# Cross-attention and FFN on one core: the last pair shuffled like the others, and half-height queries and projections

## What is computed

```
kv_rope = kv_c * cos[None] + _rotate_half(kv_c) * sin[None]
q_hk = (hidden_q @ Wq.T).reshape(b, s, H, K)
q_big = jnp.einsum('bshk,hkq->bshq', q_hk, w_kc_q)
q_r = jnp.einsum('bshq,hqr->bhsr', q_big, W_qr)
k_r = jnp.einsum('bld,hdr->bhlr', kv_rope, W_kr)
scores = jnp.einsum('bhsr,bhlr->bhsl', q_r, k_r)
attn = jax.nn.softmax(scores, axis=-1)
ctx_c = jnp.einsum('bhsl,bld->bhsd', attn, kv_rope)
ctx_lat = jnp.einsum('bhsd,hkd->bshk', ctx_c, w_kc_kv)
out = ctx_lat.reshape(b, s, H * K) @ Wo.T
```

## Time and profile before

| | |
|---|---|
| median of 3 runs | 136.69 us (136.23 to 137.05) |
| the profiled execution | 136.4 us, its span 134.6 us |
| PE busy | 127.3 us (95%) |
| DVE busy | 105.7 us (79%) |
| ACT busy | 75.5 us (56%) |
| POOL busy | 85.5 us (64%) |
| the chain that ended last | PE 75%, DVE 9%, ACT 8%, DMA 4% |

### The profile page before, as it was taken

The page is one execution under the profiler, slowest core; times in us unless marked ns, Lnnn a source line. Parts: engine busy times, 40 slices in busy tenths (PEclk is TensorE's granted clock), DMA queues, the critical chain, the costliest instruction groups (busy, mean ns, idle before and its releaser), DMA issues.

```text
span 134.6 us, 2532 instructions
## 1 busy us (share of the span) xinstructions
PE 127.3 (95%) x910; PEld 90.5 (67%) x910; DVE 105.7 (79%) x159; ACT 75.5 (56%) x192; POOL 85.5 (64%) x126
## 2 busy tenths in 40 slices
PE   6989799999889999999999999999999999999992
PEld 6767589467657767666576676666675686766770
DVE  0387844999999684996999699699969799997092
ACT  4242643769459382937638475983976673544110
POOL 6507957969989939296957959677585643004240
PEclk9999999999999999999999999999999999999999
DMA  3899987999999799899989999999889980000004
GB/s 81 232 336 216 154 135 256 231 125 211 233 252 249 150 217 211 207 297 276 245 234 305 261 249 282 239 262 309 227 234 178 267 221 23 5 0 0 0 0 156
DMA packets 29132, 26.13 MB, mean 194 GB/s; under 512 B 17056, under 2 KB 20768, under 8 KB 29120
## 3 DMA queue, kind: packets, MB, share of 16 engines
q1 hardware_dynamic: 26992, 22.84, 69.3%
q0 software_dynamic: 1456, 2.77, 9.0%
q10 hardware_dynamic: 672, 0.36, 0.9%
HBM read 10.50 MB, written 0.52 MB: 82 GB/s over the span
## 4 chain that ended last, share of the span: by engine, by line
PE 75%; DVE 9%; ACT 8%; DMA 4%; SPq 1%; issue 1%; ACTq 0%; DVEq 0%
PE score L968 18%; PE ctxb L984 16%; PE ctxb L939 8%; PE proj L994 8%; ACT probs L451 6%; DVE neg_max L650 4%; PE score L1128 4%; DMA ctx_rows<-in_ctx_dram 4%; PE foldb L904 3%; PE foldb L919 3%; DVE turned L666 2%; PE score L1153 1%; PE score L1106 1%; PE foldb L1128 1%; PE ctxb L950 1%; DVE bulk L615 1%
## 5 line engine op out<-in xcount | busy, mean ns | idle before, releaser
L451 ACT ACTIVATE probs<-score,neg_max 128x512 f32<-128x512 f32 x64 | 43.2, 686 | 28.8 <-DVE neg_max L650 28.8
L389 POOL TENSOR_SCALAR probs<-probs,row_inv 128x512 f32<-128x512 f32 x64 | 43.9, 735 | 23.8 <-DVE row_inv L656 23.8
L650 DVE TENSOR_REDUCE neg_max<-score 128x2 f32<-128x1024 f32 x32 | 37.6, 1216 | 10.9 <-PE score L968 10.9
L968 PE MATMUL score<-k_t,q_t 64*128 64x256 f32 x256 | 32.7, 391 | 1.5 <-ACT probs L451 1.4
L666 DVE STREAM_TRANSPOSE turned<-probs 128x1024 f32<-128x1024 f32 x28 | 33.0, 1216 | 0.0
L968 PEld LDWEIGHTS score<-k_t,q_t 64*128 64x128 f32 x256 | 23.2, 186 | 8.9 <-ACT probs L451 3.7
L381 POOL DMA_DIRECT2D wo<-in_L_xattn_Wo_dram x32 | 28.0, 1019 | 0.0
L984 PE MATMUL ctxb<-spread,kv 128*64 128x256 f32 x192 | 22.0, 382 | 0.0
L984 PEld LDWEIGHTS ctxb<-spread,kv 128*64 128x64 f32 x192 | 13.3, 137 | 8.0 <-issue 2.0
L939 PE MATMUL ctxb<-hq_t,m 128*128 128x512 f32 x28 | 13.7, 611 | 0.0
L451 ACT ACTIVATION_READ_ACCUMULATOR probs<-score,neg_max 128x1 f32 x64 | 13.0, 203 | 0.0
(11 more groups left out here) (144 smaller groups left out, 149.3 us busy)
## 6 DMA issues: line engine op xcount, KB each, us to landing
spread<-turned SPq DMA_DIRECT2D x56, 256.0 KB, 5.5
wo<-in_L_xattn_Wo_dram POOLq DMA_DIRECT2D x32, 64.0 KB, 5.0
wq<-in_L_xattn_Wq_dram SPq DMA_DIRECT2D x1, 1280.0 KB, 13.7
bulk<-in_L_ffn_pweight_dram SPq DMA_DIRECT2D x2, 512.0 KB, 6.2
bulk<-in_L_ffn_nweight_dram SPq DMA_DIRECT2D x2, 512.0 KB, 7.2
bulk<-in_L_xattn_w_kc_q_dram SPq DMA_DIRECT2D x4, 192.0 KB, 8.7
wq<-in_L_xattn_Wq_dram SPq DMA_DIRECT2D x1, 512.0 KB, 7.4
wkv<-in_L_xattn_w_kc_kv_dram SPq DMA_DIRECT2D x1, 512.0 KB, 5.9
```

The costliest lines, as they stand in the source:

```text
L389: pool.tensor_scalar(p, p, row_inv[:, j:j + 1], 1.0, ALU.mult, ALU.mult).then_inc(norm_made, 1)
L451: act.activation(probs[:, j, :], score[u % 2][:, h, :], ACT.Exp, bias=neg_max[:, j:j + 1], accum_out=row_sum[:, j:j + 1]).then_inc(exp_mad ...
L650: dve.tensor_reduce(neg_max[:, j:j + 2], score[u % 2][:], axis=AX, op=ALU.max, negate=True)\
L968: product = pe.matmul(score[u % 2][:, h, half * S:half * S + S], q_t[rows, i % 2, b, tt * P:tt * P + P], k_t[rows, b, half * S:half * S + ...
```

## The change

1. `key_ident`, a permuted copy of the identity, is made once on POOL. The key transposes read it in place of a permuting access pattern on `ident`.
2. For pairs 3 to 6 `queries_and_projections(i)` replaces `queries(i + 1)` and `projections(i - 3)`. Each product is split into an upper and a lower half of 64 rows, like the scores. Two halves of different batches run as a couple into different banks: query batch 0 into ctx_bank, batch 1 into fold_bank. The second couple-set adds the other halves, after a wait on PE's own semaphores. ACT takes a query with two copies (`take_split_queries`).
3. The last pair is turned by DVE and shuffled by SP like all others; kv_turned, its four transfers, the PE transposes and their copies go.
4. The FFN's scales, bias and difference move from DVE to POOL, between the normalises of pairs 5 and 6. The weighted sum stays on DVE, split in `first_bits` and `last_bits`, for output half 0 in pair 6 and before pair 7, for half 1 at the end. `weight_tanh` of half 0 comes after pair 4 in place of pair 5. The loads of Wo come a pair earlier from pair 4 on.
5. PE's order after pair 7 is new.

The core of the diff:

```diff
-            for i in range(LASTP):
+            for i in range(NP):
                 for half in range(2):
                     spread_probs(i, half)
...
+            pool.wait_ge(ident_made, 1)
+            pool.tensor_copy(key_ident[:].rearrange("p (k c) -> p k c", k=G),
+                             ident[:].rearrange("p (c k) -> p k c", k=G)).then_inc(key_ident_made, 1)
...
+            def ffn_difference(ot):
+                pool.wait_ge(tanh_made, 2 * ot + 2)
+                pool.tensor_tensor(pw[:, ot, :], pw[:, ot, :], nw[:, ot, :], ALU.subtract).then_inc(difference_made, 1)
+
             for i in range(NP):
                 for half in range(2):
                     normalise(2 * i + half)
                     for j in range(K // BK):
                         if i == 0:
                             load_wo(half, j)
-                        elif i < LASTP and j // 2 == half:
-                            load_wo(i + 1, j)
+                        elif i < SECOND and j // 2 == half:
+                            load_wo(i + 1 if i < 3 else i + 2, j)
+                            if i == 2:
+                                load_wo(4, j)
+                    if i == 5 and half == 0:
+                        weight_scales()
+                    elif i == 5:
+                        ffn_difference(0)
+                    elif i == SECOND and half == 0:
+                        bias_values()
+                    elif i == SECOND:
+                        ffn_difference(1)
...
-                if i in (5, 6):
-                    act.wait_ge(ld_ffn[i - 5], 32)
-                    weight_tanh(2 * (i - 5))
-                    weight_tanh(2 * (i - 5) + 1)
+                if i in (4, 6):
+                    act.wait_ge(ld_ffn[(i - 4) // 2], 32)
+                    weight_tanh(i - 4)
+                    weight_tanh(i - 3)
...
+            def first_bits(ot):
+
+                dve.wait_ge(difference_made, ot + 1)
+                dve.wait_ge(scales_made, 1)
                 w_bits = pw[:, ot, :].rearrange("o (i n) -> o i n", n=NB)
                 link(dve.tensor_scalar(w_ffn[:, ot, :], w_bits[:, :, 0], bits[:, 3, 0:1], None, ALU.mult))
...
+                link(dve.scalar_tensor_tensor(w_ffn[:, ot, :], w_bits[:, :, 1], bits[:, 3, 1:2],
+                                              w_ffn[:, ot, :], ALU.mult, ALU.add))
...
             for i in range(1, LASTP):
                 u, v = SLOTS * i, 2 * i
+                if i == SECOND:
+                    first_bits(0)
                 maxima(u)
...
             u, v = SLOTS * LASTP, 2 * LASTP
+            last_bits(0)
             maxima(u)
...
             early_residual(T - 1)
+            first_bits(1)
+            last_bits(1)
...
+            def queries_and_projections(i):
+
+                p, old = i + 1, i - 3
+                upper, lower = slice(0, 64), slice(64, P)
+                query_bank = [ctx_bank[:, 0:S], fold_bank[:, 0:S]]
...
+                pe.wait_ge(long_taken, contexts_count(i - 1))
+                pe.wait_ge(fold_taken, values_count(i - 1))
+                for t in range(DT):
+                    query_part(upper, t, 0, t == 0)
+                    last = query_part(lower, t, 1, t == 0)
+                last.then_inc(query_half, 1)
+                for tt in range(TT):
+                    projection_part(upper, 0, tt, old == 0)
+                    last = projection_part(lower, 1, tt, old == 0)
+                last.then_inc(projection_half, 1)
+                pe.wait_ge(query_half, old + 1)
+                for t in range(DT):
+                    query_part(upper, t, 1, False)
+                    last = query_part(lower, t, 0, False)
+                last.then_inc(long_made, 1)
+                pe.wait_ge(projection_half, old + 1)
...
+                for tt in range(TT):
+                    projection_part(upper, 1, tt, False)
+                    last = projection_part(lower, 0, tt, False)
+                last.then_inc(projected_count, 1)
...
             values_side(LASTP)
-            late_contexts(SECOND, 0)
...
+            projections(LASTP - 2)
+            late_contexts(SECOND, 0)
+            late_contexts(SECOND, 1)
+            late_project(SECOND, 0)
+            late_project(SECOND, 1)
+            late_contexts(LASTP, 0)
             pe.wait_ge(ffn_w_made, DT)
+            pe.wait_ge(long_taken, contexts_count(LASTP))
...
+            late_project(LASTP, 0)
+            late_contexts(LASTP, 1)
             transpose_hidden(0)
             transpose_hidden(1)
-            late_contexts(LASTP, 1)
             ffn(0)
-            late_project_tile(1, 0)
-            late_project_tile(1, 1)
+            late_project(LASTP, 1)
             ffn(1)
```

More of the change, by code:

```diff
@@ L580, in _ @@
                .then_inc(ffn_w_taken, 1)
-            take_hidden(0)
-            take_hidden(1)
             take_late_contexts(LASTP, 1, 4)
-            take_hidden(2)
-            take_hidden(3)
+            for t in range(T):
+                take_hidden(t)
         @block.vector
@@ L656, in inverses, with turn_two @@
                 dve.reciprocal(row_inv[:, j:j + 4], row_sum[:, j:j + 4]).then_inc(inv_made, 1)
+            def turn_two(v, n):
+                i, half, j = v // 2, v % 2, 4 * (v % 2) + 2 * n
+                if i >= 2 and n == 0:
+                    dve.wait_ge(probs_spread[i % 2][half], landed(i - 2))
+                dve.wait_ge(norm_made, 4 * v + 2 * n + 2)
+                dve.transpose(turned[i % 2][:, :, j:j + 2, :, :].rearrange("p k j l r -> p (j l) k r"),
+                              probs[:, j:j + 2, :].rearrange("p j n -> p (j n)")).then_inc(probs_turned, 1)
@@ L696, in ffn_weights, with last_bits @@
+            def last_bits(ot):
+                w_bits = pw[:, ot, :].rearrange("o (i n) -> o i n", n=NB)
+                for n in range(2, NB):
+                    link(dve.scalar_tensor_tensor(w_ffn[:, ot, :], w_bits[:, :, n], bits[:, 3, n:n + 1],
+                                                  w_ffn[:, ot, :], ALU.mult, ALU.add))
                 link(dve.bn_stats(w_stats[:, ot, :], w_ffn[:, ot, :]))
@@ L1011, in projections, with half_height, query_part, projection_part @@
                 last.then_inc(projected_count, 1)
+            def half_height(bank, stationary, moving, start, stop):
+                return pe.matmul(bank, stationary, moving, start=start, stop=stop, skip_group_check=True)
+            def queries_and_projections(i):
+                p, old = i + 1, i - 3
+                upper, lower = slice(0, 64), slice(64, P)
+                query_bank = [ctx_bank[:, 0:S], fold_bank[:, 0:S]]
+                def query_part(rows, t, b, start):
+                    return half_height(query_bank[b], m[rows, p, t, :], hq_t[rows, t, b, :], start, t == DT - 1 and not start)
+                def projection_part(rows, b, tt, start):
+                    return half_height(out_bank[b][:, tt * D:tt * D + D], ctx_t[rows, (TT * b + tt) * P:(TT * b + tt) * P + P],
+                                       n_all[rows, old, :], start and tt == 0, False)
+                pe.wait_ge(long_taken, contexts_count(i - 1))
[9 more added lines that the diff above has]
+                pe.wait_ge(query_half, old + 1)
+                for t in range(DT):
+                    query_part(upper, t, 1, False)
[6 more added lines that the diff above has]
+                last.then_inc(projected_count, 1)
             turn_keys(0)
@@ L1077, in _ @@
                 scores(i, 1)
-                queries(i + 1)
-                projections(i - 3)
+                queries_and_projections(i)
                 scores(i, 2)
```

170 lines of the change are left out of this document (51 added, 119 removed).

## The result

| | before | after |
|---|---|---|
| median of 4 runs | 136.53 us (136.23 to 137.05) | 142.12 us (141.31 to 142.78) |
| the profiled execution | 136.4 us, span 134.6 us | 142.0 us, span 140.2 us |

The ratio is 1.041, with a 95% interval of 1.038 to 1.044. The direction was forecast, but 142.12 us lies above the range of 137.0 to 141.8, and 2.6 us above the 139.5 named. In some executions of a kernel the clock is lower and the time over 1.5% longer; the medians and ratios of the experiments leave these out.

A forecast was written before the change was run, and what follows sets the result against it. PE bounds pairs 3 to 6, with little DVE slack; then DVE, ACT and PE, finally nearly all PE. Terms +6.0 - 3.6 + 0 + 0.4 = +2.8 on 136.4 gave 139.2, as a median 139.5 us; range 137.0 to 141.8.

The forecast's parts named there:

- Part 4: Pair 6: first_bits(0) on DVE waits for POOL's FFN difference, PE stands 5.2 us, and maxima(28) come 6.0 us later.
- the clock: PE work after its stand in pair 6: the clock falls to the 1.2 GHz level, costing +0.4 us.
- Part 1: Key transposes with key_ident, before the first scores: 0.87 us less PE work, bounds 0 and 0.9.
- Part 2: Half-height products in pairs 3 to 6: no change of tiling around the block, saving 0.40 us for each pair.
- Part 3: weight_tanh moved from pair 5 to pair 4 on ACT: pair 5's block waits for n_all, 0.3 us lost.
- Part 5: The end, contexts(5) to late_contexts(7, 1): 15.8 us on PE instead of 19.4, so -3.6 us.
- I take it as hidden by PE: The last pair's shuffle, landing at 124.7 to 126.9, lies under PE's work to 126.0, with up to 0.9 us to pay.
- the late bound: Last pair's shuffle: the longest time from last turn to landing, put at 8.4 us, landing at 126.9.
- The tail: Behind the start of late_contexts(7, 1): added and removed PE work cancel, change 0, 10.9 us to the end.
- heavier tail: Rival, chance 0.17: late last shuffle, longer half clock or POOL's small instructions pushing normalise(13) give 141 us.
- The half-height block doesn't pay: Rival for pairs 3 to 6, chance 0.07: couples or waits cost what the tiling change cost, +1.3 us, 140.7.
- Not slower: Rival, chance 0.16: PE's shorter end outweighs DVE's wait, for instance through faster POOL beside silent DVE; 137.1 or 135.9 us.

The follow-up runs named there:

- e2: The kernel before with key_ident alone: 136.25 us, ratio 0.998 (0.995 to 1.001).
- e5: The changed kernel with 22 products of zeros on PE before scores(6, 2), so that PE is not idle: 142.07 us, ratio 1.039.
- e3: The changed kernel with POOL's difference of output half 0 moved ahead, behind normalise(10): 137.70 us, ratio 1.009.
- e13: The kernel of e9 run once more, unchanged, for a second trace: 138.7 us, span 136.9 us.
- e9: The changed kernel with first_bits(0) moved behind pair 6, all bits of half 0 right before the maxima of pair 7: 138.8 us, ratio 1.014.
- e12: The kernel of e9 with POOL's difference of output half 1 moved behind the last normalise of pair 7: 136.75 us, ratio 1.000.
- e8: The changed kernel with first_bits(0) and last_bits(0) moved behind the last turn: 133.23 us, ratio 0.975.
- e6: The changed kernel with two of each four transfers of the last pair issued by POOL instead of SP: 143.62 us, ratio 1.051.
- e7: The changed kernel with the last pair's eight transfers moving only half their rows: 140.6 us, ratio 1.027.
- e1: The kernel before with the half-height block of pairs 3 to 6 alone: 135.66 us against 136.71, ratio 0.994.
- e10: The kernel of e8 with the old full-height queries and projections in pairs 3 to 6: 134.43 us, ratio 0.984.

## Why the prediction was right about the wait for POOL and wrong about the end

**The path to pair 7 (Part 4 and the clock): right, 1.3 us undersized.** Predicted +6.0 at maxima(28), measured 106.22 - 98.95 = +7.3. By its own steps:

- inverses(11) at 84.50, not 83.9. Most of this is Part 1: pair 3 starts 0.40 us earlier (50.79, and 51.19 before), not 0.87. One pair of traces is a poor measure of it, for in the traces of the other kernels with key_ident pair 3 starts between 50.6 and 51.6; e2 measures about 0.3, with an interval from 0.6 to nothing. Part 2's 0.40 is right for pairs 3 and 4 (11.15 against 11.53). Pair 5 takes 11.65, so Part 3 cost 0.5 us and not 0.3, 0.24 of it as a wait for n_all.
- POOL's difference: 2.4 us on the chain instead of 2.2, so it is done at 91.46 instead of 90.65. The stand of PE was 5.30 us against 5.2, and DVE's wait 6.85 against 6.7. The row of 128x256 on POOL gave the right size.
- last_bits(0): 2.80 us instead of 2.5, because L700 and L704 lay beside POOL's normalise (1.55 and 0.61 us, against 1.40 and 0.35 at the end). I had taken durations from the earlier trace rows, where POOL had nothing to do.
- the clock: 0.3 us by e5, 0.4 in the sum.

e3 shows that the wait for POOL is the cause: it takes 4.4 of the 5.6 us away. e13 (the trace of e9's kernel), e12 and e8 then sort the whole delay; their traces differ by up to 0.8 us in where pair 3 starts. Without any bits in front of pair 7 the maxima start at 97.61; with the work there but no wait, 101.28 to 102.80, depending on what POOL does beside it; with both, 106.22.

**The end (Part 5): the step that failed.** I forecast that PE gives back 3.6 us; it gives back 1.8: 129.15 - 111.42 = 17.7 us against 19.5 before. PE's own work was right: the 17.7 us hold two waits, 0.78 and 0.95, and without them they are 16.0 against 15.8. What was wrong is "I take it as hidden by PE". The last turn ended at 119.75 and the last transfer landed at 129.1, 9.35 us later, where I had bounds of 6.2 and 8.4 and paid nothing of the 0.9. (By its own terms, 3.7 of issuing and 4.9 to land, the late bound was 8.6.) The landing was not undersized: the last transfer took 4.27 us. The issuing was: the last issue started 5.1 us after the turn, at 124.84, and not 3.7. My bounds started from the turn of the last half as if SP were free. In the trace before it was, for the issue ahead of the last group ended at 103.59, just as the turn did. In pair 7 the halves are turned 2.9 us apart and four issues take 4.2 us, so SP came to the last half 1.3 us after its turn, and three issues of 0.61, 0.85 and 2.15 us passed before the last one. That SP's issues are long is not a limit of its own. In e6, with two issuers, the last issue had started 0.8 us after the turn, and the last landing still came 9.3 us after it; in e7, with half the bytes, it came 7.6 us after it. So the pace is that of the eight transfers and their bytes.

**The tail** behind late_contexts(7, 1) is 11.05 us against 10.9: right.

**The sum.** +7.3 at the maxima, -0.1 to contexts(5), -1.8 to the last contexts, +0.2 behind: +5.6. Against the forecast of +2.8 that is 0.9 at the maxima beyond the 0.4 of clock already in it, 1.8 in the end, and 0.1 in small terms.

**The rivals.** The heavier tail, at 0.17, is what happened: a late shuffle, at about double its price, and part of POOL's company; not its other causes, for the clock cost 0.3 us and POOL's nine bias instructions (100.12 to 102.55) were done before the normalise was wanted. "The half-height block doesn't pay" is refuted by e1 and e10. "Not slower" supposed that POOL beside a silent DVE runs faster. POOL's normalise took the same 2.69 us with DVE idle. The Trainium skill ("SBUF — State Buffer", section "SBUF: two separate sides") says that VectorE and GpSimd take a shared pair of ports under an exclusive lock, VectorE for an instruction in a two-port mode or with two SBUF inputs, and that the later one is blocked until the first has finished. L704 in e13 agrees, as it starts 0.24 us after POOL's instruction and ends with it, and so does e12; in which mode L704 runs no run shows. Beside the normalises, four POOL instructions in a row, the delay was smaller and on both sides: 0.2 us for each two-input product of DVE, and 0.8 us for POOL's four together. The direction in this kernel is the opposite of that rival, though: the lock costs DVE time where DVE leads, and it gave POOL nothing where DVE was silent.

**Left open.** What sets the pace of the last eight transfers was not followed. Why key_ident's 0.9 us of PE work does not reach the end was not followed. What the last pair's shuffle is worth against its PE transposes with all else equal was not run alone.

## What to carry to other kernels

Work that goes to another engine to be prepared must be asked for late: the wait stands in the queue of the engine that had no slack, and here moving the consumer behind the last critical instruction turned +4.1% into -2.5% with the same work. Time a shuffle from its first transfer to its last landing, with the transfers that are still ahead of it, and not from the moment at which its data are ready; and pay the late bound where PE's cover is under a microsecond. A duration on VectorE or GpSimd holds only with the company that it had in its row.

## What the runs showed of the hardware

- A subtraction of 128x256 on DVE (L704) took 0.35 us with POOL idle (e8, e12), 0.61 us beside a normalise (the changed kernel) and 2.25 us beside a two-input POOL instruction of 128x1024, with whose end it ended (e13). Two-input products on DVE took 0.92 and 0.88 us each beside normalises (e13) against 0.68 and 0.70 (e8).
- A two-input subtraction of 128x1024 on POOL takes 2.33 to 2.75 us (2.4 on the chain of the changed kernel), twice the 1.20 us of the same subtraction on DVE before.
- Two half-height fp32 products of different halves of the rows run together, at 0.21 us for each pair of records. The block of eight such couples took 3.46 us between two groups of scores (52.62 to 56.08), and the 0.2 us seen before at each change between full and half height are not in it.
- PE stopped at 90.18. The granted clock was still 1.00 from 93 to 94 and fell to 1.2 GHz between 94 and 95; when work began again at 95.48 it stayed there for another 6 us. It cost 0.3 us where DVE led.
- Splitting one pair's SBUF-to-SBUF transfers over SP's and POOL's queues made POOL's take a median of 7.0 us to land and SP's beside them 6.5 and 8.7 us. The last landed 9.3 us after the last turn, with eight on SP's queue alone 9.35 us.
